# Bursts of three transposed scores and blocks of 384 columns of values, in an attention kernel that ends in a gate

## The reference, cut to what matters

```python
xn = layernorm(x)
q, k, v = rope(xn @ wq + bq), rope(xn @ wk + bk), xn @ wv + bv
s = softmax(q @ k.T / sqrt(16)) @ v                       # per head
z = xn @ W.T + b;  m = sum_e p_e * (xn @ A_e) @ B_e
g = silu(z + min(0.5 * |z| / (|m| + 1e-6), 1) * m)
out = x + s * g
```

## Time and profile before

| | us |
|---|---|
| median of 3 runs (500.71 to 505.11) | 501.4 |
| the profiled execution | 500.47 |
| its span | 498.7 |
| before group 0 | 110.8 |
| group 0 | 46.0 |
| groups 1 to 6 | 272.1 |
| group 7 to its last pair of blocks | 62.0 |
| rest | 7.8 |

### The profile page before, as it was taken

The page is one execution under the profiler, slowest core; times in us unless marked ns, Lnnn a source line. Parts: engine busy times, 40 slices in busy tenths (PEclk is TensorE's granted clock), DMA queues, the critical chain, the costliest instruction groups (busy, mean ns, idle before and its releaser), DMA issues.

```text
span 498.7 us, 7226 instructions
## 1 busy us (share of the span) xinstructions
PE 464.0 (93%) x2469; PEld 186.7 (37%) x2469; DVE 374.6 (75%) x401; ACT 303.5 (61%) x593; POOL 88.6 (18%) x159
## 2 busy tenths in 40 slices
PE   8897999999999999999999999999999999999995
PEld 4573344433333333333334333333333333333331
DVE  6553788888989888888888888888888898433432
ACT  2210001237878786877877787777777787654564
POOL 8562223341010001001000100010010001012542
PEclk9997999997999999999999999999999999999999
DMA  8999844540000000000000000000000000020001
GB/s 268 272 131 126 109 68 68 72 64 1 1 1 1 3 1 3 1 1 1 1 3 0 3 0 3 1 1 3 0 3 0 3 0 3 2 75 0 28 24 44
DMA packets 13355, 17.32 MB, mean 35 GB/s; under 512 B 3089, under 2 KB 7441, under 8 KB 13329
## 3 DMA queue, kind: packets, MB, share of 16 engines
q1 hardware_dynamic: 11808, 15.84, 17.0%
q10 hardware_dynamic: 1520, 1.12, 0.8%
HBM read 6.72 MB, written 2.10 MB: 18 GB/s over the span
## 4 chain that ended last, share of the span: by engine, by line
PE 67%; ACT 13%; DVE 7%; SPq 4%; issue 4%; DMA 4%; POOL 0%; ACTq 0%; DVEq 0%
PE oT L857 26%; PE st L894 24%; ACT arena L543 13%; PE sm L797 6%; DVE negmax L612 5%; PE st L737 5%; PE sm L875 3%; SPq L288 2%; DMA kA<-arena 2%; DMA idb_sb<-in_identb 2%; PE oT L737 2%; SPq L256 1%; PE sm L878 1%; SPq L262 1%; DVE arena L594 0%
## 5 line engine op out<-in xcount | busy, mean ns | idle before, releaser
L612 DVE TENSOR_REDUCE negmax<-sm 128x1 f32<-128x1024 f32 x256 | 304.5, 1220 | 57.2 <-PE sm L797 57.0
L543 ACT ACTIVATE arena<-st 128x512 f32<-128x512 f32 x512 | 269.1, 602 | 95.9 <-PE st L894 95.3
L894 PE MATMUL st<-qA,kA 50*128 50x512 f32 x512 | 195.8, 453 | 17.9 <-ACT arena L543 11.7
L797 PE MATMUL sm<-kA,qA 48*128 48x512 f32 x512 | 199.8, 465 | 8.2 <-DVE negmax L612 4.6
L894 PEld LDWEIGHTS st<-qA,kA 50*128 50x128 f32 x512 | 85.1, 185 | 172.3 <-ACT arena L543 156.5
L857 PE MATMUL oT<-arena,vg 128*32 128x512 f32 x1024 | 138.0, 612 | 0.0
L797 PEld LDWEIGHTS sm<-kA,qA 48*128 48x128 f32 x512 | 84.4, 186 | 35.9 <-DVE negmax L612 16.8
L381 POOL TENSOR_TENSOR maxp<-negmax,consts 128x16 bf16<-128x16 f32 x16 | 3.4, 214 | 235.0 <-DVE negmax L612 235.0
L469 ACT ACTIVATE arena<-arena 128x512 fp32r<-128x512 f32 x10 | 6.3, 630 | 57.7 <-POOL arena L344 57.7
L857 PEld LDWEIGHTS oT<-arena,vg 128*32 128x32 f32 x1024 | 20.2, 108 | 34.5 <-ACT arena L543 27.1
L691 DVE TENSOR_TENSOR xT_sb<-sm,b_sb 128x512 f32<-128x512 f32 x4 | 2.8, 690 | 26.1 <-PE sm L878 26.1
(11 more groups left out here) (88 smaller groups left out, 243.8 us busy)
## 6 DMA issues: line engine op xcount, KB each, us to landing
qA<-arena SPq DMA_DIRECT2D x48, 128.0 KB, 5.1
x_sb<-in_x SPq DMA_DIRECT2D x8, 256.0 KB, 5.7
kA<-arena SPq DMA_DIRECT2D x12, 128.0 KB, 6.8
wT_sb<-in_wT SPq DMA_DIRECT2D x1, 1024.0 KB, 9.4
out<-x_sb SPq DMA_DIRECT2D x1, 896.0 KB, 4.0
out<-x_sb SPq DMA_DIRECT2D x4, 224.0 KB, 1.9
z_sb<-in_wq SPq DMA_DIRECT2D x1, 768.0 KB, 10.2
wkv<-in_wk ACTq DMA_DIRECT2D x1, 256.0 KB, 4.1
```

What stands on the lines that cost most here:

```text
L543: act.activation(probs[:, s % PB, h, :], st[:, (st_score(0, s, h) - late) % 3, :], ACT.Exp, scale=float(D) ** -0.5).then_inc(st_free, 1)
L612: dve.tensor_reduce(negmax[:, half, r:r + 1], sm[:, bank, :], AX.X, ALU.max, negate=True).then_inc(sm_free, 1)
L797: mm = pe.matmul(sm[:, bank, kh * HALF:(kh + 1) * HALF], qA[rows, half, g // 2, h, qt * P:(qt + 1) * P], kA[rows, g // 2, kh * HALF:(kh + ...
L894: pe.matmul(st[:, (st_score(0, s, h) - fewer) % 3, :], kA[rows, g // 2, kt * P:(kt + 1) * P], qA[rows, half, g // 2, h, :], start=True, st ...
```

## The change

TensorE's order in a half is no longer by key tile. The 32 pairs of a half go in 11 bursts (ten of three, the last of two). Behind a burst comes one of 10 blocks of values: the first and the last are whole key tiles of 512 columns; the 3072 columns between are cut into 8 blocks of 384 that run over the ends of key tiles (`block_parts`). Blocks 2, 3, 6 and 7 have two parts, of two key tiles, 16 records in place of 8. Block b follows burst b + 3; blocks 8 and 9 follow bursts 0 and 1 of the next half, and burst 2 has none. `pv_done` counts blocks, 20 in a group where it was 16, and ScalarE, POOL and TensorE wait for the block that completes a tile (`blocks_through`). Turned maxima stand ahead of pairs 9 and 41. Turned heads stand behind pair 11 (and 43), in front of the block. The late units of group 7 follow single pairs.

```diff
-MAX1_SLOT, MAX0_SLOT = 2, 10
+MAX1_AT, MAX0_AT = 9, 41
 OUT1_SLOT, OUT0_SLOT = 3, 11
-LAG = 2
+BURST, LAG = 3, 3
+BURSTS = -(-REP * NT // BURST)
+SPAN = 384
+BLOCKS = 2 + (NT - 2) * HALF // SPAN
 def st_score(g, s, h):
-    return ST_PER * g + 4 * s + h + (s >= MAX1_SLOT) + (s >= MAX0_SLOT)
+    i = 4 * s + h
+    return ST_PER * g + i + (i >= MAX1_AT) + (i >= MAX0_AT)
 def st_max1(g):
-    return ST_PER * g + 4 * MAX1_SLOT
+    return ST_PER * g + MAX1_AT
 def st_max0(g):
-    return ST_PER * g + 4 * MAX0_SLOT + 1
+    return ST_PER * g + MAX0_AT + 1
+def block_parts(b):
+    if b in (0, BLOCKS - 1):
+        return [(0 if b == 0 else NT - 1, 0, HALF)]
+    at, end = HALF + SPAN * (b - 1), HALF + SPAN * b
+    cut = min(end, (at // HALF + 1) * HALF)
+    return [(a // HALF, a % HALF, a % HALF + z - a) for a, z in ((at, cut), (cut, end)) if z > a]
+def blocks_through(g, s):
+    kt = s % NT
+    return 2 * BLOCKS * g + BLOCKS * (s // NT) + (BLOCKS if kt == NT - 1 else 1 - (-kt * HALF // SPAN))
 def sm_base(g):
...
+LATE_UNITS = {2: [(4, 0), (4, 1)], 5: [(4, 2), (4, 3)], 8: [(4, NE)], 11: [(5, 0)], 14: [(5, 1), (5, 2)],
+              17: [(5, 3), (5, NE)], 20: [(6, 0), (6, 1)], 23: [(6, 2), (6, 3)], 26: [(6, NE), (7, 0)],
+              29: [(7, 1), (7, 2)], 31: [(7, 3)], 34: [(7, NE)]}
 def build(nc, x, wq, wk, wv, biases, bv, wT, b, A, B, p_sc, cosT, sinT, ident, identb, ones, out):
...
             def evacuate(g, half, n, free):
-                act.wait_ge(pv_done, 16 * g + 8 * (half + 1))
+                act.wait_ge(pv_done, blocks_through(g, NT * half + NT - 1))
                 if free is not None:
                     act.wait_ge(sm_full, free)
                 act.activation(heads[:, half, :], oT[:, :], ACT.Copy).then_inc(heads_out, 1)
             def step(g, first=False, last=False):
                 for s in range(16):
...
                         if h == 0 and not (first and s < PB):
-                            act.wait_ge(pv_done, 16 * g + s - PB + 1)
+                            act.wait_ge(pv_done, blocks_through(g, s - PB) if s >= PB
+                                        else blocks_through(g - 1, s - PB + 16))
...
-                        if s == LAG - 1 and h == 1 and not first:
+                        if (s, h) == (1, 1) and not first:
                             evacuate(g - 1, 1, 2 * g - 1, sm_base(g - 1) + 2 * OUT1_SLOT + 1)
-                        if s == 8 + LAG - 1 and h == 1:
+                        if (s, h) == (9, 1):
                             evacuate(g, 0, 2 * g, None if first else sm_out0(g - 1) + 1)
             step(0, first=True)
...
-            def values(g, s, exps, free):
-                kt = s % NT
-                pe.wait_ge(st_free, exps)
-                if kt == 0:
-                    if free is None and s == 0:
+            def values(g, half, b):
+                s = NT * half + block_parts(b)[-1][0]
+                fewer = 1 if g == LAST and 4 * s + 3 >= MAX0_AT else 0
+                pe.wait_ge(st_free, st_score(g, s, 3) + 1 - fewer)
+                if b == 0:
+                    if (g, half) == (0, 0):
                         claim_bank(3)
-                    if free is not None:
-                        pe.wait_ge(heads_out, free)
-                    if s == 0:
+                    else:
+                        pe.wait_ge(heads_out, 2 * g + half)
+                    if half == 0:
                         pe.wait_ge(v_ready, g + 1)
-                for h in range(REP):
-                    mm = pe.matmul(oT[h * VC:(h + 1) * VC, :], vg[:, g % 2, kt, :], probs[:, s % PB, h, :],
-                                   start=(kt == 0), stop=(kt == NT - 1))
+                for kt, first_col, end_col in block_parts(b):
+                    cols = slice(first_col, end_col)
+                    for h in range(REP):
+                        mm = pe.matmul(oT[h * VC:(h + 1) * VC, cols], vg[:, g % 2, kt, :],
+                                       probs[:, (NT * half + kt) % PB, h, cols],
+                                       start=(kt == 0), stop=(kt == NT - 1))
                 mm.then_inc(pv_done, 1)
...
-            def step(g, first=False, last=False):
-                for s in range(16):
-                    half, kt = s // NT, s % NT
-                    rows = slice(ROWS * (g % 2), ROWS * (g % 2) + KM)
-                    fewer = 1 if last and s >= MAX0_SLOT else 0
-                    def score_cols(h):
-                        n = st_score(g, s, h) - fewer
-                        if first and s == 0 and h < 3:
-                            claim_bank(h)
-                        else:
-                            pe.wait_ge(st_free, n - 2)
-                        pe.matmul(st[:, (st_score(0, s, h) - fewer) % 3, :],
-                                  kA[rows, g // 2, kt * P:(kt + 1) * P], qA[rows, half, g // 2, h, :],
-                                  start=True, stop=True).then_inc(st_full, 1)
...
-                    if s == OUT1_SLOT and not first:
+                    fewer = 1 if last and i >= MAX0_AT else 0
+                    n = st_score(g, s, h) - fewer
+                    if first and i < 3:
+                        claim_bank(i)
+                    else:
+                        pe.wait_ge(st_free, n - 2)
+                    pe.matmul(st[:, n % 3, :], kA[rows, g // 2, kt * P:(kt + 1) * P], qA[rows, half, g // 2, h, :],
+                              start=True, stop=True).then_inc(st_full, 1)
+                    if not last:
+                        e = 2 * s + h // 2
+                        n = sm_score(g, e, first)
+                        score_rows(g + 1, e, n % 2, n - 1, (h % 2,))
+                    if i % (REP * NT) % BURST != BURST - 1 and i % (REP * NT) != REP * NT - 1:
+                        continue
+                    if i == 4 * OUT1_SLOT - 1 and not first:
                         n = SM_LAST["out1"] if last else sm_out1(g)
-                        turn_heads(1, (n if last else sm_out1(0)) % 2, 2 * g, n - 1)
-                    if s == OUT0_SLOT:
+                        turn_heads(1, n % 2, 2 * g, n - 1)
+                    if i == 4 * OUT0_SLOT - 1:
                         n = SM_LAST["out0"] if last else sm_out0(g)
-                        turn_heads(0, (n if last else sm_out0(0)) % 2, 2 * g + 1, n - 1)
-                    score_cols(0)
-                    next_rows(2 * s, 0)
-                    score_cols(1)
-                    next_rows(2 * s, 1)
-                    if s >= LAG:
-                        at = s - LAG
-                        values(g, at, st_score(g, at, 3) + 1 - (1 if last and at >= MAX0_SLOT else 0),
-                               None if first and at == 0 else 2 * g + at // NT)
-                    elif not first:
-                        at = s - LAG + 16
-                        values(g - 1, at, st_score(g - 1, at, 3) + 1, None)
+                        turn_heads(0, n % 2, 2 * g + 1, n - 1)
+                    b = (burst - LAG) % BURSTS
+                    if burst >= LAG:
+                        values(g, half, b)
+                    elif b < BLOCKS and half == 1:
+                        values(g, 0, b)
+                    elif b < BLOCKS and not first:
+                        values(g - 1, 1, b)
                     if last:
-                        for unit in LATE_UNITS.get(s, ()):
+                        for unit in LATE_UNITS.get(i, ()):
                             late_unit(*unit)
-                    score_cols(2)
-                    next_rows(2 * s + 1, 0)
-                    score_cols(3)
-                    next_rows(2 * s + 1, 1)
-            step(0, first=True)
```

More of the change, by code:

```diff
@@ L390, in group_values @@
                 if g >= 2:
-                    pool.wait_ge(pv_done, 16 * (g - 1))
+                    pool.wait_ge(pv_done, 2 * BLOCKS * (g - 1))
                 pool.tensor_tensor(vg[:, g % 2, :, 0:D], v_sb[:, :, cols],
@@ L520, in step @@
                 for s in range(16):
[L521 to L533, removed]
-                    for h in range(REP):
-                        late = 1 if last and s >= MAX0_SLOT else 0
+                    for h in range(REP):
+                        if 4 * s + h == MAX1_AT:
+                            act.wait_ge(st_full, st_max1(g) + 1)
+                            if not first:
+                                act.wait_ge(max_in, 16 * 2 * g)
+                            act.activation(maxT[:, 1, :], st[:, st_max1(0) % 3, :].bitcast(BF16)[0:32, 0:P],
+                                           ACT.Copy).then_inc(st_free, 1)
+                        if 4 * s + h == MAX0_AT and not last:
+                            act.wait_ge(st_full, st_max0(g) + 1)
+                            act.wait_ge(max_in, 16 * (2 * g + 1))
+                            act.activation(maxT[:, 0, :], st[:, st_max0(0) % 3, :].bitcast(BF16)[0:32, 0:P],
+                                           ACT.Copy).then_inc(st_free, 1)
```

(44 more changed lines are left out.)

3 lines of the change are left out of this document (removed).

## The result

The changed kernel takes 528.3 us (median of 4 runs, 526.54 to 528.44) against 503.2; the ratio of the runs is 1.049, 95% interval 1.043 to 1.056. Slower by 5%, and outside my range of 490 to 511. The profiled execution took 528.23, its span is 526.4.

What follows compares the result with a forecast made beforehand. It took a loop between TensorE and ScalarE as the bound, VectorE close behind. 500.47 + 0.5 (13 halves) + 1.4 (group 0) - 3.6 (group 7) = 498.8 us profiled, 499.7 as median; range 490 to 511.

Steps and rivals of the forecast that it cites:

- What bounds the kernel, and what is late next: Groups 0 to 6: TensorE's wait for ScalarE, 0.37 us per four pairs, goes; rows of scores waiting for VectorE come next.
- The loop of the cut row tile: Mid-half: a row tile split by a block waits for its bank and VectorE; 4.18 us for six pairs, against 3.92 before.
- the walk from block 8 to block 1: From block 8 to block 1 of the next half, walked step by step: 8.89 us.
- A whole half: Sum over one half: 8.36 + 5.32 + 8.89 = 22.57 us, taken as 22.72 with two-part blocks and hand-overs; 22.68 before.
- the turned heads wait for tile 4's bank: Before block 0 of a half: heads wait for VectorE's reduction of row tile 4, until 6.40 us after block 8's start.
- Rival D: Group 0 stays at the low clock for longer; another low stretch costs about 3 us, total 503; chance 0.08.
- Group 7: Last group, without rows of scores: 5.6 us gained from the fourth pair's wait, less 1.2 and 0.8, so -3.6.
- Two-part blocks: Blocks 2, 3, 6 and 7 of each half: extra time for spanning two key tiles, taken as 0.1 us each.
- e: Extra time of one two-part block over a one-part block: taken as 0.1 us, between nothing and 0.99.
- rival C: Two-part blocks in every half are costly: at 0.5 us extra each the total is 516 us; chance 0.18.
- my forecast of no change: Whole kernel: the wait for ScalarE replaced by one for VectorE of the same size; 499.7 us, chance 0.62.
- Halves of 22.4 to 23.1: Sign to check in groups 1 to 6: each half stays within 22.4 to 23.1 us.

## Why the prediction was wrong

**What bounds the kernel, and what is late next: right.** The loop of the cut row tile was put at 4.18 for six pairs. In the kernel with four added matmuls the blocks of a half start so:

```profile
211.01 0.85 PE L883 MATMUL oT<-arena,vg 128*32 128x384 f32 x8
...
215.19 0.86 PE L883 MATMUL oT<-arena,vg 128*32 128x256 f32 x16
...
219.39 0.85 PE L883 MATMUL oT<-arena,vg 128*32 128x384 f32 x8
...
224.70 0.53 PE L883 MATMUL oT<-arena,vg 128*32 128x384 f32 x4
```

Block 1 to 3 to 5: 4.18 and 4.20, then 5.31 to block 8, forecast 5.32. In the changed kernel itself they are 4.19 and 4.19. The half at full clock is 22.67, forecast 22.72.

**The step that failed** is the walk from block 8 to block 1 in "A whole half". I walked it at full clock: 8.89. The changed kernel took 209.93 to 220.22, 10.29; with four added matmuls, at full clock, it is 9.00. The difference, 1.3, is the half clock from 215.9 to 219.3. I had written down the very wait whose addition brings lows back, "the turned heads wait for tile 4's bank", and priced it by its length only. Over 12 halves this is 290.67 - 271.99 = 18.7 us: eleven lows of 3.4 us at about 1.4, and the one of 10.2 us at 3.4.

**Rival D** named the low clock, but in group 0 alone, once, 3 us at 0.08. The place was wrong: every half of groups 1 to 6 has it. Group 0 took 49.3; with the four added matmuls 46.5, where I had 46.0 + 1.4. That term was also added up wrongly: two pairs more at 0.49 are 1.0 and not 1.5, which would have made it 0.8.

**Group 7.** Forecast -3.6. The kernel with four added matmuls seems to confirm it, 66.3 against 69.8 before, but its eight added matmuls in group 7 find no wait to fill and cost about 1.6. The same order at full clock stands in the run with whole row tiles alone: 37.10 + 27.55 = 64.65, so -5.1. The sign is right and the gain too small: the 0.8 for two-part blocks is nearly nothing (below), and 0.7 stays open. In the changed kernel the low clock over the second half puts 10.6 on top, 75.3. This is the second step that failed, a term that the prediction had at nothing. Unlike in groups 1 to 6 no wait explains it, and its cause stays open.

**Two-part blocks.** I took e = 0.1, bounds 0 and 0.99. Before the next first pair a one-part block lasts 0.78 and a two-part one 0.79, e is about 0.01 and rival C is dead. The rule that a change of tiling mode drains the engine, and a change of tile alone doesn't (the Trainium skill, TensorEngine Tiling (Array Packing), Key Properties) fits: the cost of a block's ends does not grow with its parts, which share one mode.

**Sum.** From the kernel with four added matmuls to the changed one, 493.7 to 526.4: 18.7 in groups 1 to 6, 9.0 in group 7 (10.6 less the 1.6 of the added matmuls), 2.9 in group 0, and 2.1 before it, where the two kernels are alike. At full clock my forecast of no change would have held (ratio 0.996), in part because group 7 gained more than I had; the clock made it 5% slower.

**What would show it.** I asked for ScalarE's wait to shrink to a small part; it only halved. Rows of scores waiting for the maxima were to become TensorE's largest wait; at 35.1 us they are less than half of that (they were 16.8 before), while single ones reach the 0.8 that I had. So VectorE took over part of the role, not all. "Halves of 22.4 to 23.1" was the test that failed, and the line of the granted clock on the page showed why at once.

## What to carry to other kernels

A wait is not priced by its length alone where TensorE is thinly used around it: 0.7 us of waiting cost 1.3 us more at the low clock, per half. Put the instruction that waits behind the densest work at hand, not in front: one swapped call was worth over 30 us here, of which some 10 in group 7 are not explained by the wait. Read the granted clock stretch by stretch before pricing anything else. When a burst pattern replaces another, lay it over every stream that shares the engine; bursts of three freed the scores and cut the row tiles, and the one paid for the other until the rows were regrouped too.

## What the runs showed of the hardware

The granted clock fell to 1.2 GHz although the longest idle stretch of TensorE near it was 0.72 us, of which 0.3 lay ahead of the fall, with a busy share of 2.84 / 3.30 in the stretch ahead. The second half of group 7 lost the clock in the changed kernel and kept it in the run with whole row tiles, whose instructions there are the same. Added matmuls helped in one place (four inside a wait, clock 1.00) and did not in another (two between pairs, 498 to 590 us). And the low clock can hold on through dense work, 23.8 us in group 7 and 41 of group 0's 58.6 us with whole row tiles and the heads behind, where TensorE shows 97% busy.
